# Summing the absolute weights on another engine, and loading them from another queue

## The reference

```python
def _quant_weight(w):
    scale = jnp.mean(jnp.abs(w)) + EPS
    wq = jnp.clip(jnp.round(w / scale), -1.0, 1.0)
    return (wq, scale)

gate = jax.nn.silu(_qlinear(x, w_gate))
up = _qlinear(x, w_up)
return _qlinear(gate * up, w_down)
```

## Time and profile before

| what | us |
|---|---|
| median of 10 runs | 9924.36 |
| the runs, lowest to highest | 9897.81 to 9951.26 |
| the profiled execution, its time | 9930.87 |
| its span on the slowest core (core 3) | 9929.3 |
| stage 1, about | 0 to 740 |
| stage 2, about | 740 to 4400 |
| the tail | 4400 to 4676 |
| stage 3 to the end | 4676 to 9929 |

### The profile page before, as it was taken

One profiled execution on the slowest core, in us unless ns is written; L12 is line 12 of the kernel. 1 busy time (PEld: TensorE's weight loads), 2 busy tenths in 40 slices (PEclk: granted clock), 3 DMA queues, 4 the chain that ended last, 5 costly groups with the idle time before them and its releaser, 6 DMA issues.

```text
span 9929.3 us, 105893 instructions; the slowest of 8 cores (9840.3 to 9929.3 us)
## 1 busy us (share of the span) xinstructions
PE 5663.2 (57%) x29954; PEld 2956.1 (30%) x29954; DVE 3012.4 (30%) x6433; ACT 2517.1 (25%) x7191; POOL 300.5 (3%) x555
## 2 busy tenths in 40 slices
PE   2232344555556666640645767766776775565757
PEld 1111123333444444430212222222322232222222
DVE  2323333333333333320123433433433422112020
ACT  4443334433444444443001111111111120000000
POOL 0000000000000000000000000000000001111212
PEclk7665555555555555555767878888888888888989
DMA  6453111111100000325243333333333324444444
GB/s 157 147 163 69 45 39 33 37 39 28 28 26 24 20 28 24 56 66 157 107 138 99 101 102 101 100 100 103 99 103 104 99 79 134 138 130 143 127 138 127
DMA packets 367329, 883.65 MB, mean 89 GB/s; under 512 B 44977, under 2 KB 122930, under 8 KB 352306
## 3 DMA queue, kind: packets, MB, share of 16 engines
q1 hardware_dynamic: 194114, 503.50, 16.0%
q10 hardware_dynamic: 129024, 268.49, 9.1%
q0 software_dynamic: 43632, 104.89, 5.0%
HBM read 755.07 MB, written 159.39 MB: 92 GB/s over the span
## 4 chain that ended last, share of the span: by engine, by line
DMA 33%; PE 27%; DVE 17%; issue 13%; ACT 5%; DVEq 3%; SPq 1%; ACTq 1%; another core or an unknown queue 1%; POOL 0%; POOLq 0%
DMA wpre<-wgT 8%; DMA wpre<-wdT 8%; DMA csb<-wdq_s 7%; DMA wpre<-wuT 6%; PE pE L632 4%; DVE pbuf L637 3%; PE pA L533 3%; PE pC L650 3%; PE pD L650 3%; DVE xbuf L894 2%; DVE atb L897 2%; PE pA L776 2%; DVE hmaxp L983 2%; PE pA L480 2%; DVEq L982 1%
## 5 line engine op out<-in xcount | busy, mean ns | idle before, releaser
L894 DVE TENSOR_SCALAR xbuf<-wpre,wsinv 128x512 f32<-128x512 f32 (+1 forms) x640 | 344.5, 538 | 1627.2 <-DMA wpre<-wdT 631.5
L971 ACT ACTIVATE xbuf<-xbuf 128x512 f32<-128x512 f32 x256 | 161.1, 629 | 2297.0 <-DVE hmaxp L983 2294.9
L632 PE MATMUL pE<-identb,pbuf 128*128 128x128 bf16 x3200 | 425.1, 306 | 452.2 <-DVE pbuf L615 445.4
L533 PE MATMUL pA<-ktdup,tb 64*128 64x128 bf16 x2176 | 356.0, 299 | 568.6 <-ACT pbuf L570 551.2
L269 PE MATMUL pE<-identb,tb 128*128 128x128 bf16 x896 | 99.5, 279 | 848.2 <-DVE tb L1063 345.6
L247 ACT ACTIVATE pjunk<-wpre 128x1024 bf16<-128x1024 f32 x384 | 405.7, 1056 | 692.6 <-DMA wpre<-wgT 313.1
L1107 PE MATMUL pA<-csb,ktdup 128*128 128x512 bf16 x1024 | 400.1, 391 | 304.7 <-DMA csb<-wdq_s 228.6
L637 DVE COPY pbuf<-pE 128x1024 bf16<-128x1024 bf16 (+7 forms) x512 | 294.4, 575 | 914.5 <-PE pE L632 844.0
L555 ACT ACTIVATE negb<-mh 128x1 f32<-128x1 f32 x512 | 102.7, 201 | 1780.7 <-DVEq L552 1780.7
L570 ACT ACTIVATE pbuf<-pA,negb 128x512 bf16<-128x512 f32 (+3 forms) x768 | 486.8, 634 | 64.8 <-PE pA L533 25.2
L632 PEld LDWEIGHTS pE<-identb,pbuf 128*128 128x128 bf16 x3200 | 302.9, 136 | 559.6 <-issue 559.6
(11 more groups left out here) (163 smaller groups left out, 9126.0 us busy)
## 6 DMA issues: line engine op xcount, KB each, us to landing
wpre<-wgT ACTq DMA_DIRECT2D x128, 512.0 KB, 5.3
wpre<-wuT ACTq DMA_DIRECT2D x128, 512.0 KB, 4.1
wpre<-wdT ACTq DMA_DIRECT2D x128, 512.0 KB, 4.5
wpre<-wgT SPq DMA_DIRECT2D x256, 256.0 KB, 3.2
wpre<-wuT SPq DMA_DIRECT2D x256, 256.0 KB, 3.3
wpre<-wdT SPq DMA_DIRECT2D x128, 512.0 KB, 4.5
h_s<-f32a SPq DMA_DIRECT2D x256, 256.0 KB, 2.1
csb<-wdq_s POOLq DMA_DIRECT2D x512, 128.0 KB, 2.7
```

The costliest lines, as they stand in the source:

```text
L533: e.matmul(d2, q2, ktdup[p2 * 64:p2 * 64 + 64, (h2 // 4) * 2048 + jj * 128: (h2 // 4) * 2048 + (jj + 1) * 128], start=True, stop=True),
L632: w.run("T", lambda e, kk=k, g=g0, b2=bank: e.transpose(b2[:, kk * 128:(kk + 1) * 128], pf[:, (g + kk) * 128:(g + kk + 1) * 128], identb[: ...
L894: w.run("V", lambda e, s2=slot, q2=qa, ws=wsel, n3=n2: e.tensor_scalar(q2, s2[:, 0:n3], wsinv[:, ws:ws + 1], MAGIC, ALU.mult, ALU.add))
```

## The change

The slices are summed by DVE in place of ACT, and loaded by POOL in place of ACT. The sum is one `reduce_sum` with absolute values; before it was an `activation` with `Abs` and an accumulator. The two slots are handed back by DVE's semaphore, and the loads use the semaphores `dD2` and `dD3`. The number of slices, the two slots and the places in the text at which `prepass_step` is called stay. A `drain` is added on DVE ahead of the final sums.

```diff
-        pre = {"iss": 0, "done": 0, "ld": [], "absS": [0, 0]}
+        pre = {"iss": 0, "done": 0, "ld": [], "absV": [0, 0]}
...
-                    sn = "dP%d" % (k % 2)
-                    w.wait("S", sn, c[sn])
-                    w.wait("S", "sS", pre["absS"][k % 2])
-                    w.run("S", lambda e, s=slot, r=src: e.dma_start(s, r),
-                          inc=sn, incn=16)
+                    sn = "dD%d" % (2 + k % 2)
+                    w.wait("G", "sV", pre["absV"][k % 2])
+                    dma("G", slot, src, sn)
...
-                w.wait("S", pre["ld"][kd][0], pre["ld"][kd][1])
-                w.run("S", lambda e, s=slot, cc=col, kp=kd % 2: e.activation(
-                    pjunk[:, kp * 1024:kp * 1024 + 1024], s, AF.Abs,
-                    accum_out=wsums[:, cc:cc + 1]), inc="sS")
-                pre["absS"][kd % 2] = c["sS"]
+                w.wait("V", pre["ld"][kd][0], pre["ld"][kd][1])
+                w.run("V", lambda e, s=slot, cc=col: e.reduce_sum(
+                    wsums[:, cc:cc + 1], s, axis=AXX,
+                    apply_absolute_value=True), inc="sV")
+                pre["absV"][kd % 2] = c["sV"]
...
         w.wait("V", "sS", c["sS"])
+        w.run("V", lambda e: e.drain())
```

## The result

The changed kernel takes 10354.57 us (median of 9 runs, 10332.42 to 10395.90) where the kernel before takes 9923.24 (32 runs): a ratio of 1.0436, 95% interval 1.0417 to 1.0454. The forecast was 10,290 in a range of 10,165 to 10,400. The direction and nearly all places were right; one term was three times too small.

The account below looks back on a forecast made before the run. No engine was busy over 57% of the span, so waits between engines counted. Terms 220 + 21 + 24 + 34 + 34 + 34 = 367 on 9930.87 gave 10,298, less 6.5 over the median: 10,290 us, range 10,165 to 10,400.

Parts of the forecast that it names:

- The place of the sums: In stage 1 eight sums stand uncovered between DVE's last copy and the next tile's first sum, 21.55 us.
- stage 1: DVE's uncovered bursts, less ACT's lateness and a short idle, cost 14.66 us a tile for 15 tiles: +220.
- hidden sums: Rival: DVE's sums fall into its idle time and ACT's bursts go for nothing, 9,760 us; chance 0.02.
- The slot cycle: Load, sum and hand over of one slot take 6.4 us, entering 96 times: the tail and 16 bursts.
- the tail: After stage 2, 48 pairs of slices at 6.4 us each end at 4709.95 against 4675.80: +34.
- Quick landings: Rival: slice loads land in 3.6 us with no hand over, a cycle of 4.8 us, 10,145 us; chance 0.10.
- POOL starved: Rival: POOL must wait out a DVE sum to write descriptors, a cycle of 7.6 us, 10,405 us; chance 0.08.
- Queue order of wq and wo: On POOL, wq before stage 2 and wo before stage 3 stand behind slice loads: +21 and +34.
- Heads: Stage 2: three bursts a tile cost 1.93 us each, first bursts 0.15, and ACT's 70.6 go: +24.
- The 70.6 of the kernel before: Stage 2, ACT's bursts: each tile's first to last bias less 31 ordinary heads, over 16 tiles, in us.
- Between tiles: Stage 2: SP waits for two more sums before loading the next input, 2.27 us at 15 boundaries: +34.
- The rest: Everything behind stage 3's first tile, forecast to change by 0.

Follow-up runs that it names:

- e10: The changed kernel with three slots, SP's wait ahead of the fifth burst's sums, and stage 1's sums moved to DVE's idle places: 9867.84 us, ratio 0.9975.
- e5: The changed kernel with the four wo loads moved in POOL's order to right behind tile 15's query projection: 10374.85 us, ratio 1.0483.
- e6: The changed kernel with the wq load moved in POOL's order ahead of the slice loads of stage 1's last burst: 10342.17 us, ratio 1.0444.
- e2: The changed kernel with the slices loaded by ACT in place of POOL, still summed by DVE: 10318.35 us, ratio 1.0386.

## Why the prediction was right, and which term was mis-sized

- **The place of the sums (right).** Every burst stands bare on DVE, as worked out from the order; e10 shows the same sums nearly free in DVE's gaps of stage 1. The rival "hidden sums" failed by its place, not by its idea.
- **The slot cycle (right, 6.23 for 6.4).** It carries stage 1 and the tail: +206 and +30 where 220 and 34 were put. "Quick landings" (4.8) and "POOL starved" (7.6) both fall; the Trainium skill (SBUF — State Buffer, Who interferes with whom) says that a reduction does not lock POOL out, and the trace agrees, with 0.53 us for an issue during a sum. (The 10,145 of "quick landings" was taken from 10,298; from the forecast of 10,290 it is 10,136.)
- **Queue order of wq and wo (right).** +18.5 and +37 for 21 and 34; e5 gives wo's 37 back. That wq's 18.5 is the queue's order rests on its issue at 961.73, behind a slice's load that waits for a sum; e6 does not show it. That an earlier issue gains nothing in e5 and e6 was no part of the prediction.
- **Heads (right in size, in part by luck).** The three later bursts of a tile cost 2.2 us each where I had 1.93 (mean of all tiles and cores), 107 for 93, and none falls into slack. Yet the excess over ordinary heads, taken as in the prediction, is about 85 us, not 95. What I left out is a tile's first step, from its first bias to its second: no earlier head's scaling and copies stand in it, and it is 2.2 us shorter than an ordinary one, not 0.15 longer. The 70.6 of the kernel before has that in it and the 95 has not. The two errors nearly cancel in +16 for +24.
- **Between tiles (the mis-sized term: 34, measured 101).** The failed step is "The `csb` loads stand behind slices too, but land before the first rotation". That is true and answers the wrong question. I asked whether csb comes late for its reader, not whom its transfer slows. The two sums let csb, two slices and the next input go at almost one moment, and the input needs 3.9 us more than it used to. The order of POOL's loads stood in sight. The price of company did not: the load of 3.60 us in the earlier trace rows had another issued beside it, at 252.27, so it does not show what a load takes alone.
- **The rest (+27, put at 0).** The later stages run the same instructions. The term goes with the queue of the slices all the same: the four kernels that load them from ACT take 5177 to 5183 us here, the nine that load them from POOL 5197 to 5232, though no slice of the pre-pass is loaded in this stretch. The granted clock does not part them (0.84 in the first group, 0.83 to 0.84 in the second). What makes them differ stays open.

The forecast came in 65 us low, and the gaps' 67 us make up nearly all of it. The errors of the other terms, -26 together, and the +27 of the rest cancel, which is luck.

## What to carry to other kernels

A moved step is priced by what stands behind it on its new engine: two sums of 1.2 us cost 2.2 in a head, six cost under 1 in an idle place, and a pair cost a whole slot's cycle where the loads were not ahead. When a wait is added, list everything that the same event releases; those transfers start together and slow the one on the path. And where a ring of slots sets the pace, more slots are the remedy: a third was worth 1.6% of the time before on DVE and 2.0% on ACT. The choice of the loads' queue alone came out even here, but only as a balance of losses and gains.

## What the runs showed of the hardware

- Two 512 KB loads issued on POOL within 2 us behind the 8 MB of wq landed only with it, some 54 us on; a slice of the same size from ACT's queue, beside the same wq, landed in 12.6 us (e2), and loads from SP beside POOL's were slowed (4.93 to 8.85 us) but not held up so.
- POOL takes 0.61 to 0.62 us from the end of DVE's sum to the start of the load that it releases, in nearly all turns of the changed kernel; with two slots that is a tenth of the cycle.
